# Heads of self and cross turned by DMA transposes as f16 halves, two query biases moved to ScalarE, all orders rewritten

## The chip, the cores and the metric

The kernel runs on one core of one Trainium2 chip. The metric is the device time of one execution in microseconds. TensorE (PE) multiplies, VectorE (DVE) and GpSimd (POOL) do elementwise work, ScalarE (ACT) evaluates functions, and SyncE (SP) issues the DMAs.

## The reference

Two attention blocks in a row over 64 sequences of 64 rows, width 256, 16 heads of 16. Cut to its core:

```python
# block L0: x, encoder_states = ctx
ln = layernorm(x); q, k, v = split(ln @ w_qkv + b_qkv)
x = x + merge(softmax(mask(q k / 4)) v) @ w_ao + b_ao            # "self"
q = layernorm(x) @ w_q + b_q; k, v = split(ctx @ w_kv + b_kv)
x = x + merge(softmax(mask(q k / 4)) v) @ w_co + b_co            # "cross"
x = x + gelu(layernorm(x) @ w1 + b1) @ w2 + b2                   # "mlp0"
# block L1: latents = x; keys of ctx ("ctx") and of the latents ("lat") share one softmax
h = concat([ctx, x]); q = x @ q_w + q_b; k, v = (h @ kv_w + kv_b)
y = softmax(mask(q k / 16)) v @ out_w + out_b + x                # "lat"
out = gelu(rmsnorm(y) @ mlp_w1 + mlp_b1) @ mlp_w2 + mlp_b2 + x   # "mlp1"
```

## The kernel before

The 4096 rows are cut into 32 units of 128 rows, two sequences each. Every unit goes through the same stages: self, cross, mlp0, ctx and lat, mlp1. Most large products are made of three f16 products: a matrix is kept as a high f16 half and a low f16 half (value minus high half). The weights are scaled and halved once, in the first part of the program.

Each engine has its own program, and each program is a list of stage calls written out by hand: a start (all engines fill up), a loop `for t in range(FILL, SLOTS)` and an end. One pass of the loop does each stage once, but for different units: `mix(t - 2, "self")` stands beside `hidden(t - 6, "mlp1", ...)`. The engines run these lists strictly in order and meet only at semaphores, so an instruction that waits holds up all that stands behind it on its engine. FILL is 6 before, so the loop has 26 passes.

The stages around the change, for t = self or cross, unit u:

- `mix` (PE, L609): probabilities times values into a PSUM bank. `denominators` and `divided` (DVE, L1249 and L1256) divide and write `heads_t` to SBUF as f32, 128 rows by 256 features.
- `heads_turn` (PE, L455): two f32 128x128 transposes of `heads_t` into PSUM. `heads_out` (ACT, L1823) casts the result to the high half, `heads_low` (DVE, L1156) subtracts it from PSUM and writes the low half. For lat, `heads_out` copies f32 and there are no halves.
- `project` (PE, L482; for lat L624): the turned heads times the output weight. `add_residual` (DVE, L1270, lat L1267) follows.
- `q_bias_self`, `q_bias_cross`, `q_bias_lat` (DVE, through `descaled`, L1149): query from PSUM, scale and bias, one instruction of 128x256 each. `score` (PE, L576) reads it.
- `gelu` (ACT, L1867), `hidden_hi` (ACT, L1876) and `hidden_lo` (DVE, L1276) make the halves of the hidden layer. `exponential` (ACT, L1853) makes the probabilities. Gelu and exponential use different function tables; the compiler puts an ACT_TABLE_LOAD where the program goes from one to the other.
- `across` (SP, L2498): a DMA transpose that turns a pair of f16 halves of normalized rows, `pair_t`, into `turned_t`. Before, five of them are issued for every unit (self, cross, mlp0, lat, mlp1); `load_x`, `load_rest` (four DMAs) and `store` are issued by SP too.

## Time and profile before

| | before |
|---|---|
| median of 3 runs | 1120.4 us (1119.05 to 1125.32) |
| profiled execution, device time | 1117.1 us |
| its span | 1115.1 us |
| granted TensorE clock, mean of the span | 0.991 |
| PE busy / DVE busy / ACT busy / POOL busy | 1037.7 / 982.0 / 785.7 / 633.9 us |

The span is the time from the first to the last instruction; the device time is 2.0 us more. The busy time of an engine is the union of its instructions. Ends of matmuls are modelled, so a short wait on PE can hide in busy time. In a list of waits the left side waited for the right side. In the chain that ended last, each piece is what held up the piece after it.

### The profile page before, as it was taken

How to read it: one execution, taken by the hardware profiler on the slowest of the kernel's cores; microseconds unless marked ns; L12 is line 12 of the kernel's file. 1: busy time of each engine (PE TensorE's matmuls, PEld its weight loads, DVE VectorE, ACT ScalarE, POOL GpSimd, SP SyncE). 2: the span in 40 equal slices, each digit the busy share in tenths (PEclk: the TensorE clock that was granted, in tenths of full speed). 3: DMA queues.
4: the chain of work that ended last, by engine and by line, in shares of the span. 5: the costliest groups of instructions: out<-in, count | busy, mean ns of one | idle time of the engine just before them, and what ended most of it. 6: DMA issues, size and time to landing. Idle time of an engine off the chain costs nothing.

```text
span 1115.1 us, 46381 instructions
## 1 busy us (share of the span) xinstructions
PE 1037.7 (93%) x19304; PEld 908.9 (82%) x19304; DVE 982.0 (88%) x2360; ACT 785.7 (70%) x1773; POOL 633.9 (57%) x903
## 2 busy tenths in 40 slices
PE   6677899999999999999999999999999999999997
PEld 5666678888888888888888888888888888878786
DVE  3888979989989999899999989999999999889774
ACT  2446677877667777777677777766777777666786
POOL 3866666555556565655565656555665566464421
PEclk9898999999999999999999999999999999999999
DMA  9541111122111121221111111111111122110111
GB/s 316 175 146 47 46 28 29 33 43 43 38 34 35 39 37 34 43 43 36 33 38 37 39 34 43 43 33 31 43 33 34 43 43 43 32 28 17 26 30 31
DMA packets 117473, 55.09 MB, mean 49 GB/s; under 512 B 98960, under 2 KB 115088, under 8 KB 116240
## 3 DMA queue, kind: packets, MB, share of 16 engines
q1 hardware_dynamic: 117264, 52.13, 19.4%
q8 instruction: 153, 2.51, 0.9%
q14 instruction: 56, 0.46, 0.1%
HBM read 26.93 MB, written 4.19 MB: 28 GB/s over the span
## 4 chain that ended last, share of the span: by engine, by line
PE 45%; DVE 23%; DMA 12%; ACT 10%; issue 6%; POOL 2%; SPq 1%; ACTq 0%; POOLq 0%; DVEq 0%
PE psum L469 11%; PE psum L649 10%; PE psum L609 7%; PE psum L482 6%; DMA turned_lat<-pair_lat 5%; PE psum L595 5%; DMA turned_cross<-pair_cross 4%; PE psum L576 4%; ACT staging L1867 2%; ACT hid_mlp L1867 2%; DVE prob_self L1214 2%; DVE prob_cross L1243 2%; PE psum L455 2%; DVE mx_ctx L1224 2%; DVE prob_cross L1214 1%
## 5 line engine op out<-in xcount | busy, mean ns | idle before, releaser
L2270 POOL TENSOR_TENSOR prob_self<-prob_self,add_self 128x512 f32<-128x512 f32 x64 | 90.9, 1437 | 87.8 <-DVE prob_self L1214 87.7
L2270 POOL TENSOR_TENSOR prob_cross<-prob_cross,add_cross 128x512 f32<-128x512 f32 x64 | 81.1, 1288 | 59.9 <-DVE prob_cross L1214 59.9
L2219 POOL TENSOR_TENSOR rstd_mlp<-var_mlp,minus_half 128x1 f32<-128x1 f32 x64 | 36.3, 567 | 123.1 <-DVE var_mlp L1137 89.8
L1867 ACT ACTIVATE hid_mlp<-psum,folded,undo_in 128x128 f32<-128x128 f32 x256 | 95.8, 464 | 7.2 <-PE psum L469 7.2
L1867 ACT ACTIVATE staging<-psum,cols,undo_in 128x128 f32<-128x128 f32 x256 | 96.2, 457 | 4.9 <-PE psum L469 3.9
L649 PE MATMUL psum<-hi_n,staging 128*128 128x256 f16 x512 | 94.3, 273 | 1.2 <-DVE staging L1276 1.2
L469 PE MATMUL psum<-turned_mlp,hi_m 128*128 128x128 f16 x1024 | 92.7, 219 | 2.4 <-DMA turned_mlp<-pair_mlp 2.1
L469 PE MATMUL psum<-turned_mlp,hi_n 128*128 128x128 f16 x1024 | 92.5, 219 | 0.3 <-DMA turned_mlp<-pair_mlp 0.3
L649 PE MATMUL psum<-hi_m,parts_mlp 128*128 128x256 f16 x512 | 90.1, 273 | 1.1 <-DVE parts_mlp L1276 1.1
L469 PE MATMUL psum<-turned_mlp,lo_n 128*128 128x128 f16 x512 | 88.9, 219 | 0.0
L469 PE MATMUL psum<-turned_mlp,lo_m 128*128 128x128 f16 x512 | 88.9, 219 | 0.0
L1853 ACT ACTIVATE probT_cross<-psum 128x512 f32<-128x512 f32 x64 | 35.1, 595 | 73.4 <-PE psum L595 73.3
L1853 ACT ACTIVATE late<-psum 128x512 f32<-128x512 f32 x128 | 69.7, 596 | 22.0 <-PE psum L595 21.5
L2247 POOL TENSOR_TENSOR xb<-x,rows 128x256 f32<-128x256 f32 x96 | 84.5, 881 | 0.2
L469 PEld LDWEIGHTS psum<-turned_mlp,hi_m 128*128 128x128 f16 x1024 | 76.8, 98 | 8.2 <-issue 6.6
L469 PEld LDWEIGHTS psum<-turned_mlp,hi_n 128*128 128x128 f16 x1024 | 79.6, 98 | 1.8 <-DMA turned_mlp<-pair_mlp 0.6
L2276 POOL TENSOR_TENSOR late<-late,mx_ctx 128x512 f32<-128x512 f32 x64 | 70.4, 1101 | 17.7 <-DVE mx_ctx L1230 14.8
L649 PE MATMUL psum<-lo_n,staging 128*128 128x256 f16 x256 | 69.8, 273 | 0.0
L649 PE MATMUL psum<-lo_m,parts_mlp 128*128 128x256 f16 x256 | 69.8, 273 | 0.0
L1853 ACT ACTIVATE probT_self<-psum 128x512 f32<-128x512 f32 x64 | 35.0, 595 | 44.3 <-PE psum L595 44.3
L469 PE MATMUL psum<-turned_lat,hi_side 128*128 128x128 f16 x512 | 49.6, 219 | 16.9 <-DMA turned_lat<-pair_lat 16.9
L609 PE MATMUL psum<-val_ctx,late 128*64 128x34 f32 x1024 | 62.2, 225 | 0.3 <-issue 0.3
(267 smaller groups left out, 3801.5 us busy)
## 6 DMA issues: line engine op xcount, KB each, us to landing
xin<-in_x SPq DMA_DIRECT2D x32, 128.0 KB, 2.3
late<-in_ctxT SPq DMA_DIRECT2D x4, 1024.0 KB, 7.6
ctxT<-in_ctxT SPq DMA_DIRECT2D x32, 128.0 KB, 2.1
late<-in_x SPq DMA_DIRECT2D x4, 1024.0 KB, 6.2
out<-xb SPq DMA_DIRECT2D x32, 128.0 KB, 1.9
staging<-in_w_m SPq DMA_DIRECT2D x2, 1024.0 KB, 7.2
staging<-in_w_n SPq DMA_DIRECT2D x2, 1024.0 KB, 5.2
mask<-in_mask_cross SPq DMA_DIRECT2D x32, 32.0 KB, 1.9
```

Source lines behind the costliest of these rows:

```text
L469: last = e.matmul(out_ap, wt[name][:, k, c:c + P], xs[:, k, :], start=(n == 0), stop=(n == 3 * KH - 1))
L482: last = e.matmul(ps[:, 0:H], xs[:, k, :], wt[name][:, k, c:c + H], start=(n == 0), stop=(n == 3 * KH - 1))
L576: last = e.matmul(ps[here, h * HC * S:(h + 1) * HC * S], qT["lat" if t == "ctx" else t][rows_of, h, here], spread[t][rows_of, h, :, here], ...
L595: last = e.transpose(bank[in_bank["prob_turn", t, a, u]][:, n * S:(n + 1) * S], prob[t][h][here, j * P:(j + 1) * P], ident[here, here])
L609: last = e.matmul(ps[S * a:S * a + S, p * VW:(p + 1) * VW], probT[s][a][:, j, :], val[s][:, a, p, :], start=(n == 0), stop=(n == len(sets) ...
L649: last = e.matmul(ps[:, 0:H], a, wt, start=(g == 0 and n == 0), stop=(g == 1 and n == 11))
L1853: e.activation(probT[t][a][:, :, :], src, ACT.Exp).then_inc(sem["probT_" + t], 1)
L1867: last = e.activation(hid[t][g][:, j * P:(j + 1) * P], ps[:, j * P:(j + 1) * P], ACT.Gelu_apprx_tanh, bias=b1[:, 4 * g + j:4 * g + j + 1], ...
L2219: e.tensor_tensor(rstd[t][:, :], var[t][:, :], minus_half[:, :], ALU.pow).then_inc(sem["rstd_" + t], 1)
L2247: e.tensor_tensor(o[:, :], a[:, :], row, ALU.add).then_inc(sem["plus_bias_" + t], 1)
L2270: e.tensor_tensor(ch, ch, over_heads(a[:, :]), ALU.add).then_inc(sem["added_" + t], 1)
L2276: e.tensor_tensor(ch, ch, over_keys(max_of("ctx", h)), ALU.subtract).then_inc(sem["shifted_ctx"], 1)
```

## The change

For self and cross, the heads are halved before they are turned. ACT casts `heads_t` to f16 (`heads_high`), DVE subtracts that from `heads_t` in SBUF (`heads_low`), and SP turns both halves with one DMA transpose (`heads_across`); `project` waits for that DMA. `heads_turn` and `heads_out` stay for lat alone. `q_bias_cross` and `q_bias_lat` move to ACT as two instructions each. FILL becomes 7, and every list, of start, loop and end, is written in a new order. The core of the diff, without the lists:

```diff
-FILL, SLOTS = 6, UNITS
+FILL, SLOTS = 7, UNITS
...
+        heads_pair = {t: sb("heads_pair_" + t, [P, 2, H], F16) for t in ("self", "cross")}
+        heads_turned = {t: sb("heads_turned_" + t, [P, 2, KH, P], F16) for t in ("self", "cross")}
...
                     q.wait_ge("lo_side", 1)
-                    q.wait_ge("heads_lo_" + t, u + 1)
+                    q.wait_ge("heads_across_" + t, 16 * (u + 1))
...
             def heads_low(u, t):
-                ps = bank[in_bank["heads_turn", t, u]][:, 0:KH * P].rearrange("p (k t) -> p k t", k=KH)
-                q.wait_ge("headsT_" + t, u + 1)
-                e.tensor_tensor(h_lo[t], ps, h_hi[t], ALU.subtract).then_inc(sem["heads_lo_" + t], 1)
+                q.wait_ge("heads_hi_" + t, u + 1)
+                e.tensor_tensor(heads_pair[t][:, 1, :], heads[t][:, :], heads_pair[t][:, 0, :], ALU.subtract).then_inc(sem["heads_lo_" + t], 1)
...
+            def heads_high(u, t):
+                q.wait_ge("heads_" + t, 2 * u + 2)
+                q.wait_ge("heads_across_" + t, 16 * u)
+                e.copy(heads_pair[t][:, 0, :], heads[t][:, :]).then_inc(sem["heads_hi_" + t], 1)
...
+            def q_bias_cross(u):
+                q.wait_ge("q_mm_cross", u + 1)
+                q.wait_ge("score_cross", u)
+                q.wait_ge("undone", UNDONE["out"])
+                ps = bank[in_bank["q", "cross", u]]
+                for k in range(KH):
+                    last = e.activation(qT["cross"][:, k, :], ps[:, k * P:(k + 1) * P], ACT.Identity, bias=folded[:, 6 + k:7 + k], scale=down_q[:, 1:2])
+                last.then_inc(sem["q_cross"], 1)
...
+            def heads_across(u, t):
+
+                q.wait_ge("heads_lo_" + t, u + 1)
+                q.wait_ge("proj_mm_" + t, u)
+                q.wait_ge("heads_across_" + t, 16 * u)
+                e.dma_start_transpose(heads_turned[t][:, :, :, :].rearrange("p i k t -> p (i k) t"),
+                                      heads_pair[t][:, :, :].rearrange("p i h -> p (i h)")).then_inc(sem["heads_across_" + t], 16)
```

On TensorE, in a pass in the middle of the loop, the transposes of the lat's and self's heads stood right behind the mix of self and ahead of other work. Before:

```order
L609 MATMUL psum<-val_self,probT_self 64x34 x16
L576 MATMUL psum<-spread_ctx,q_lat 64x128 x16
L455 MATMUL psum<-ident,heads_lat 128x128 x2
L455 MATMUL psum<-ident,heads_self 128x128 x2
L482 MATMUL psum<-hi_side,turned_lat 128x256 x4
L482 MATMUL psum<-lo_side,turned_lat 128x256 x2
```

After, the projection of cross comes behind `qk_self`, `v_self` (the first two rows) and two turns of probabilities; the mixes of cross and self stand some 34 rows further up:

```order
L482 MATMUL psum<-hi_qkv,turned_self 128x256 x4
L482 MATMUL psum<-lo_qkv,turned_self 128x256 x2
L596 MATMUL psum<-ident,late 128x64 x32
L482 MATMUL psum<-hi_out,heads_turned_cross 128x256 x4
L482 MATMUL psum<-lo_out,heads_turned_cross 128x256 x2
```

So the two transposes of self's heads are gone, and between the mixes and the projections stands the lat's projection, one half of `hidden`, `qk_self`, `v_self` and two `prob_turn`.

On ScalarE, one stretch of a loop pass with all gelus and the loads of function tables. Before (`staging` is the hidden layer of mlp1, `late` the scores of ctx and lat):

```order
L1867 ACT_TABLE_LOAD
L1867 ACTIVATE staging<-psum,cols,undo_in 128x128 x4
L1845 ACTIVATE val_lat<-psum,undo 64x8x16 x4
L1808 ACTIVATE xn_cross<-x,shift_cross,rstd_cross 128x256
L1876 ACTIVATE staging<-staging,hidden_up 128x512
L1867 ACTIVATE staging<-psum,cols,undo_in 128x128 x4
L1867 ACTIVATE hid_mlp<-psum,folded,undo_in 128x128 x4
L1876 ACTIVATE parts_mlp<-hid_mlp,hidden_up 128x512
L1867 ACTIVATE hid_mlp<-psum,folded,undo_in 128x128 x4
L1816 ACTIVATE pair_mlp<-xb,rstd_mlp 128x256
L1876 ACTIVATE parts_mlp<-hid_mlp,hidden_up 128x512
L1853 ACT_TABLE_LOAD
```

After, behind three gelus of the same pass:

```order
L1938 ACT_TABLE_LOAD
L1938 ACTIVATE probT_self<-psum 128x512
L1930 ACTIVATE val_lat<-psum,undo 64x8x16 x4
L1938 ACTIVATE probT_self<-psum 128x512
L1938 ACTIVATE probT_cross<-psum 128x512 x2
L1915 ACTIVATE pair_lat<-x,power 128x256
L1961 ACTIVATE staging<-staging,hidden_up 128x512
L1887 CAST heads_pair_cross<-heads_cross 128x256
L1930 ACTIVATE val_cross<-psum 64x8x16 x4
L1887 CAST heads_pair_self<-heads_self 128x256
L1952 ACT_TABLE_LOAD
L1952 ACTIVATE staging<-psum,cols,undo_in 128x128 x4
```

The exponentials of self and cross now lie between the third and the fourth gelu, so a pass has four table loads instead of two; the program has 120 instead of 68.

On SyncE, one pass of its queue. Before:

```order
L2498 DMA_TRANSPOSE turned_cross<-pair_cross 128x4x128
L2506 DMA out<-xb 128x256
L2498 DMA_TRANSPOSE turned_lat<-pair_lat 128x4x128
L2498 DMA_TRANSPOSE turned_mlp<-pair_mlp 128x4x128
L2498 DMA_TRANSPOSE turned_self<-pair_self 128x4x128
L2465 DMA xin<-in_x 128x256
L2498 DMA_TRANSPOSE turned_mlp<-pair_mlp 128x4x128
```

After:

```order
L2616 DMA xin<-in_x 128x256
L2666 DMA out<-xb 128x256
L2649 DMA_TRANSPOSE turned_self<-pair_self 128x4x128
L2649 DMA_TRANSPOSE turned_lat<-pair_lat 128x4x128
L2658 DMA_TRANSPOSE heads_turned_cross<-heads_pair_cross 128x4x128
L2658 DMA_TRANSPOSE heads_turned_self<-heads_pair_self 128x4x128
L2628 DMA ctxT<-in_ctxT 128x256
L2629 DMA mask<-in_mask_cross 128x64
L2631 DMA keys_i<-in_mask_keys 64x64 x2
L2649 DMA_TRANSPOSE turned_mlp<-pair_mlp 128x4x128 x2
L2649 DMA_TRANSPOSE turned_cross<-pair_cross 128x4x128
```

A pass has seven transposes instead of five. The loads of ctx and masks now stand behind the two turns of heads.

## Rows read from the trace of the kernel before

**Rows 1.** The page, part 1: busy time, share, instructions of each engine.

```profile
PE 1037.7 (93%) x19304; PEld 908.9 (82%) x19304; DVE 982.0 (88%) x2360; ACT 785.7 (70%) x1773; POOL 633.9 (57%) x903
```

**Rows 2.** Busy time by stretch: length, busy us (instructions) by engine, PEclk, DMA, GB/s.

```profile
200.00:1000.00 800.00, 775.15 (x14818) 682.21 (x14802) 739.39 (x1771) 587.39 (x1349) 468.43 (x649) 1.00 0.18 38
```

**Rows 3.** heads_self on VectorE, asked at 190:215 and at 1000:1035.

```profile
L1256 DVE TENSOR_TENSOR heads_self<-psum,over_self x1: 424/424/424, 199.9 to 199.9; 128x256 f32<-128x256 f32 x1
...
L1256 DVE TENSOR_TENSOR heads_self<-psum,over_self x2: 424/424/425, 1001.0 to 1028.5; 128x256 f32<-128x256 f32 x2
```

**Rows 4.** Waits of TensorE's weight load, 200:1000: us, times, longest.

```profile
PEld psum L469 <- DMA turned_lat<-pair_lat: 18.2, 12, 1.8
...
PEld psum L469 <- DMA turned_cross<-pair_cross: 10.7, 12, 1.8
...
PEld psum L455 <- DVE heads_self L1256: 0.4, 2, 0.2
```

**Rows 5.** Waits of VectorE, 200:1000.

```profile
DVE headsT_cross L1156 <- ACT headsT_cross L1823: 18.5, 12, 1.8
...
DVE headsT_self L1156 <- ACT headsT_self L1823: 7.2, 25, 0.3
...
DVE mx_lat L1224 <- PE psum L576: 0.5, 1, 0.5
```

**Rows 6.** Waits of ScalarE, 200:1000.

```profile
ACT probT_cross L1853 <- PE psum L595: 63.9, 25, 2.6
...
ACT late L1853 <- PE psum L595: 19.7, 26, 1.9
```

**Rows 7.** Chain that ended last, 560:660: start, us, what.

```profile
560.55 2.98 DMA turned_cross<-pair_cross
...
564.43 0.66 PE psum L482 x6
565.08 0.65 PE psum L595 x16
...
581.25 0.67 PE psum L469 x12
...
636.83 4.31 DMA turned_lat<-pair_lat
```

**Rows 8.** Timeline of TensorE, around 615: start, duration, instruction.

```profile
615.05 0.43 PE L455 MATMUL psum<-ident,heads_self 128*128 128x128 f32 x2
615.32 0.60 PE L482 MATMUL psum<-hi_side,turned_lat 128*128 128x256 f16 x4
```

**Rows 9.** Timeline of ScalarE, 616 to 620.

```profile
616.52 1.28 ACT L1867 ACT_TABLE_LOAD   x1
617.82 1.50 ACT L1867 ACTIVATE staging<-psum,cols,undo_in 128x128 f32<-128x128 f32 x4
619.20 1.51 ACT L1845 ACTIVATE val_lat<-psum,undo 64x128 f32<-64x128 f32 x4
```

**Rows 10.** Groups by line and shape: busy us, mean ns | idle before, releaser.

```profile
L1149 DVE SCALAR_TENSOR_TENSOR q_cross<-psum,down_q,folded 128x256 f32<-128x256 f32 x32 | 15.3, 478 | 10.9 <-PE psum L469 10.5
...
L1156 DVE TENSOR_TENSOR headsT_cross<-psum,headsT_cross 128x256 f16<-128x256 f32 x32 | 13.6, 424 | 23.4 <-ACT headsT_cross L1823 21.8
...
L1146 DVE TENSOR_TENSOR pair_mlp<-xn_mlp,pair_mlp 128x256 f16<-128x256 f32 x32 | 24.2, 757 | 1.3 <-POOL pair_mlp L2228 1.3
...
L1830 ACT ACTIVATE pair_lat<-x,power 128x256 f16<-128x256 f32 x32 | 16.3, 510 | 1.8 <-DVE x L1286 1.8
...
L1823 ACT CAST headsT_cross<-psum 128x256 f16<-128x256 f32 x32 | 11.9, 372 | 50.7 <-PE psum L455 50.6
...
L1867 ACT ACT_TABLE_LOAD x34 | 43.6, 1283 | 0.6
```

**Rows 11.** Timeline of SyncE's queue: start, time of the issue.

```profile
638.12 2.39 SPq L2498 DMA_TRANSPOSE turned_mlp<-pair_mlp  x1
```

**Rows 12.** Tile turned_lat: time to landing over 32 transposes.

```profile
DMA to landing us min/median/max: 2.4/2.5/4.6
```

More of the change, by code:

```diff
@@ new lines, in _ @@
+            total(0, "n2", 5)
+            q_cross(2, 3)
+            project(1, "cross", 1)
+            score(2, "cross", 2)
+            hidden(0, "mlp0", 1, 4)
+            outward(0, "mlp0", 0, 7)
+            qk_self(5, 2)
+            k_cross(3, 5)
+            outward(0, "mlp0", 1, 7)
+            prob_turn_bank(2, "cross", 1)
+            mix(4, "self", 6)
+            prob_turn(2, "cross", 7)
+            project(3, "self", 4)
+            score_bank(5, "self", 2)
+            score(5, "self", 0)
@@ L762, in _ @@
+            mix(2, "cross", 4)
+            hidden(1, "mlp0", 0, 2)
+            hidden(1, "mlp0", 1, 7)
+            q_lat(0, 4)
+            score_bank(0, "ctx", 2)
+            k_lat(0, 6)
+            score(0, "ctx", 4)
+            v_self(5, 0)
+            v_cross(3, 1)
             score_bank(0, "lat", 4)
             score(0, "lat", 2)
-            total(0, "n2", 1)
-            q_cross(3, 6)
-            project(2, "cross", 0)
-            outward(1, "mlp0", 0, 1)
+            k_ctx(1, 6)
@@ new lines, in _ @@
+            v_self(UNITS - 1, 0)
+            q_cross(UNITS - 2, 2)
+            score_bank(UNITS - 1, "self", 4)
+            score(UNITS - 1, "self", 6)
+            heads_turn(UNITS - 5, "lat", 1)
+            score_bank(UNITS - 2, "cross", 2)
+            score(UNITS - 2, "cross", 4)
+            hidden(UNITS - 6, "mlp1", 0, 1)
+            k_lat(UNITS - 4, 6)
+            v_ctx(UNITS - 4, 3)
+            hidden(UNITS - 3, "mlp0", 0, 0)
+            project(UNITS - 5, "lat", 2)
+            hidden(UNITS - 3, "mlp0", 1, 7)
@@ L1952, in _ @@
             exponential(0, "lat", 1)
-            exponential(4, "self", 1)
+            normalize(2, "mlp0")
+            exponential(3, "cross", 0)
+            heads_out(0, "lat")
+            exponential(3, "cross", 1)
+            q_bias_lat(1)
+            values(1, "ctx")
             gelu(2, "mlp0", 0)
+            heads_high(3, "cross")
+            hidden_hi(2, "mlp0", 0)
+            gelu(2, "mlp0", 1)
+            hidden_hi(2, "mlp0", 1)
             values(1, "lat")
-            heads_out(0, "lat")
@@ L2006, in _ @@
-            heads_out(UNITS - 5, "lat")
-            gelu(UNITS - 6, "mlp1", 1)
+            values(UNITS - 4, "ctx")
+            gelu(UNITS - 3, "mlp0", 0)
+            gelu(UNITS - 3, "mlp0", 1)
+            exponential(UNITS - 1, "self", 0)
+            exponential(UNITS - 1, "self", 1)
+            hidden_hi(UNITS - 3, "mlp0", 0)
+            hidden_hi(UNITS - 3, "mlp0", 1)
+            exponential(UNITS - 2, "cross", 0)
+            heads_high(UNITS - 1, "self")
+            exponential(UNITS - 2, "cross", 1)
@@ L2016, in _ @@
[L2016 to L2023 removed]
+            normalize(UNITS - 1, "cross")
+            q_bias_lat(UNITS - 3)
+            gelu(UNITS - 6, "mlp1", 1)
+            normalize(UNITS - 2, "mlp0")
```

1865 lines of the change are left out of this document (988 added, 877 removed).

## The prediction

> **What bounds the kernel now.** I read the shares first: PE 93%, DVE 88%, ACT 70%, POOL 57% [rows 1]. Shares mix the start, where weights are loaded and halved, with the loop, so next came the stretch 200 to 1000, which is nothing but the loop, at full granted clock (1.00, the 2.4 GHz level): PE busy 775.2 of 800 us, DVE 739.4, ACT 587.4 [rows 2]. The reader should see that two engines are nearly full and a third is not.
>
> The length of a pass is read from one instruction that occurs once in it. heads_self starts at 199.9 for one unit and at 1001.0 for the unit 25 passes on [rows 3]: 801.1 / 25 = 32.04 us a pass. The other 314 us of the span are start and end.
>
> What would a pass be without waits? The waits by engine answer that. TensorE's weight load waited for others in six groups, from 18.2 to 0.4 us and 39.4 in all, 1.58 a pass; the two largest, together 28.9, are for the DMA transposes of the lat's and of cross's rows [rows 4]. That leaves 32.04 - 1.58 = 30.46 us of PE. DVE waited 43.3 us in five groups, 18.5 to 0.5, so 1.73 a pass; its own work is 30.31. Most of that waiting is heads_low for ACT, 18.5 and 7.2 [rows 5]. ACT waited 205 us in six groups from 63.9 to 19.7 and a last one of 0.2, so 8.2 a pass, and holds 23.84 us of work [rows 6]. So a pass of 32.04 is a PE of 30.5 and a DVE of 30.3, both in written order, plus about 1.6 us that PE loses, mostly to landings. The chain shows what such a landing is: 2.98 us from the end of DVE's low half for cross at 560.55, but 4.31 for the lat's at 636.83 [rows 7], where the next transpose stands right behind and its issue took 2.39 us [rows 11]. Over all 32, the lat's landed in 2.4 to 4.6 us, median 2.5 [rows 12]. That median counts from the issue's end, the chain's pieces from its start.
>
> **The change part by part, per pass.**
>
> TensorE. Two pairs of f32 transposes go. One pair occupies from 615.05 to 615.32, where the next matmul starts [rows 8]: 0.27 us, not the 0.43 shown, since matmuls overlap. Two pairs are 0.54, and PE's own work falls from 30.46 to 29.92. No other product changes.
>
> VectorE. Two query biases of 478 ns go [rows 10]: -0.96, less a little because neighbours overlap, which I leave out. heads_low now has two SBUF inputs in place of one in PSUM. Its old form took 424 ns; the nearest rows of the new form are the low halves of normalized rows, of which mlp0's take 757 ns [rows 10]. So it costs between nothing and 2 x 0.33 = 0.67; I take 0.35, as POOL is busy little over half the time. DVE's work is then 30.31 - 0.96 + 0.35 = 29.7 (29.35 to 30.0). The 757 ns row stands at a place where POOL adds rows at the same time. The Trainium skill, SBUF — State Buffer, section Who interferes with whom, says that a DVE instruction with two SBUF inputs contends with a GpSimd instruction that reads SBUF; by it alone either bound could come out, depending on what POOL does then, so the sum goes by the rows.
>
> ScalarE. Two more table loads: the load at 616.52 is followed by the gelu at 617.82, so 1.30 each, 2.60 in all [rows 9]. Four bias instructions of 128x128 from PSUM, with scale and bias from SBUF: a gelu of the same shape and operands goes four in 1.38 us (617.82 to 619.20) [rows 9]; I take 1.38, and 2.04 as the upper bound at the 510 ns of pair_lat, which has more columns. Below 1.38 I see no reason. Two heads_high at 510 replace two casts of 372: +0.28 [rows 10]. Sum 23.84 + 2.60 + 1.38 + 0.28 = 28.1, at most 28.8. That is hidden under PE's 29.9 if ACT waits for no more than 1.8 us a pass, where it now waits 8.2. So this cover is thin: three engines of 29.9, 29.7 and 28.1 have to mesh.
>
> The table loads are the place where a rule speaks against the change. The Trainium skill, ScalarE: Activation LUTs, section What ACT_TABLE_LOAD costs, has 1283 ns for the load and about 1380 for a drain, 2.66 for each switch. The trace has the 1283 [rows 10] and, from load to next gelu, 1.30 with no further gap. By the page's figure two more switches would be an estimated 5.3 us and ACT the bound at 30.9 before any wait; by the row they are 2.6.
>
> The new wait. project now waits for a DMA. Behind it on PE stand q_lat and all else; so what matters is the work between mix and project. For self it is, by the order, the lat's projection, 24 matmuls of hidden, 24 of qk_self, v_self, two turns of probabilities, cross's projection and q_lat. 12 such matmuls take 0.67, six of 256 columns 0.66, a turn of probabilities 0.65 [rows 7]: 4 x 0.67 + 2 x 0.66 + 2 x 0.65 + 0.67 = 6.0, without the lat's projection. The chain to be hidden is reciprocal and divide (about 0.7, an estimate from the 424 ns form and a small one before it), heads_high 0.51, heads_low 0.42 to 0.76, and the landing at 2.98 to 4.31: 4.6 to 6.3. Usual landings are hidden; a slow one just about. The two heads' transposes lie back to back in SP's list, the pattern that gave 4.31. Cross is first there and has the same distance.
>
> Old landings. The DMAs that PE waited for get room. lat_low stands in DVE's new list ahead of the division of cross's heads, so it is done when the mix of cross is; q_lat comes on PE only behind the lat's projection, 48 matmuls of hidden and qk_self, v_self, two turns and cross's projection: over 5.3 us by the same rows. Cross's rows are turned at the end of DVE's pass and q_cross stands behind 48 hidden matmuls of the next, 2.7 us. load_rest's four DMAs now stand behind the heads' and not in front of lat's and cross's. So of the 28.9 us / 25 = 1.16 a pass I expect 1.0 to go and 0.15 to stay. The other 0.42 (10.5 us / 25) are waits for ACT and DVE; I let them stay, as those two engines get fuller relative to PE.
>
> Pass after: 29.92 + 0.15 + 0.42 = 30.5. If DVE takes its upper bound 30.0, this still holds.
>
> SP. Seven transposes at no more than the 2.39 us of a blocked one [rows 11] are under 17 us of issue in a pass of 30: no bound, but each waits in line.
>
> Start and end. Seven units' share of transposes lies there: 7 x 0.54 = -3.8. At the end nothing covers the landings of the last self and cross heads: each replaces 0.27 + 0.37 by 2.98 and more, about +2.5, so +5. FILL 7 moves one pass from the loop into the written-out start; it is one pass of the same work. I cost the new order of the first loads at nothing, with 10 us either way as its bound.
>
> **Sum.** 25 x (30.5 - 32.04) = -38.5; -3.8 + 5 = +1.2. Span 1115.1 - 37.3 = 1077.8; the device time is 2.0 more, 1079.8. The profiled execution was 3.3 below the median of the runs, whose three values spread over 6 us; I stay with **1080**.
>
> **The rivals.**
>
> 1. Half a gain (chance 0.22). In-order engines at 29.9, 29.7 and 28.1 don't mesh: a late exponential or a late q_bias holds up PE, or slow landings of the seven transposes go on. For it: ACT's 1.8 us of room, the 4.31. Against: DVE's waits for headsT, 25.7 us of its 43.3, are gone. With a pass of 31.2: 25 x 0.84 = 21; 1117.1 - 21 + 1 = 1097.
> 2. All waits go (0.07). Pass 29.9: 25 x 2.14 = 53.5; 1117.1 - 53.5 + 1 = 1065.
> 3. The gain doesn't arrive (0.06). New waits eat all that old ones gave back, pass 32.0: 1117 to 1122. This would be the change that doesn't do what it says: landings late as before, only of heads in place of lat's.
> 4. Slower (0.07). ACT becomes the bound, by the split of gelus and exponentials. If ACT has its upper 28.8 and keeps half of its present 8.2 us of waits, since it must wait in order for PE's turns of probabilities, a pass is 32.9 and the time 1117.1 + 25 x 0.86 + 1 = 1139. It decides from 32.04 - 28.1 = 3.9 us of ACT waiting a pass on. Against it: in the new order exponentials stand behind several pieces of ACT work that can be done meanwhile. The skill's 2.66 per switch (same page as above) would push the same way, to an estimated pass of 32 to 33; the trace has no such drain at either kind of switch.
>
> The forecast itself, 1066 to 1094, has 0.58.
>
> **How the numbers follow.** A measurement of this kernel can tell about 0.5% (5.6 us) from no change. Forecast, rival 1 and rival 2 are faster: 0.87. Rival 3 is the same: 0.06. Rival 4 is slower: 0.07. The range 1062 to 1106 leaves out rivals 3 and 4 (0.13), the upper part of rival 1 and little below; it holds the start's 10 us either way around 1080 and the pass between 29.9 and 31.5.
>
> **What the profile after would show.** Right: L455 with lat alone, 64 instead of 192 transposes; a pass of 30.2 to 30.8 us by the same instruction's starts; PE's waits for turned_lat and turned_cross under 5 us each in the loop; ACT busy near 910 (785.7 + 67 + 44 + 9) with 120 table loads of 1.28; DVE busy near 960; heads_low between 0.42 and 0.76. Wrong in part: project (L482) waiting for heads_turned by more than 10 us in the loop, which says slow landings; PE waiting for probT or late (L1938) by more than 25, which is rival 1 or 4 by ACT. Wrong altogether: a gap of over 1 us behind each table load, or a start longer by over 10 us than 200 us less one pass's gain, which the loop could not make good.

## The result, and the profile after

| | before | after |
|---|---|---|
| median | 1120.28 us (1119.05 to 1125.32, 4 runs) | 1105.09 us (1103.1 to 1106.9, 4 runs) |
| profiled execution, span | 1115.1 us | 1104.4 us |

The ratio is 0.9856, 95% interval 0.9819 to 0.9892: faster by 15 us, where 40 were forecast. The time lies in the range, 1 us from its slow end, and 8 us behind rival 1 (half a gain, 1097), whose pass of 31.2 us it has.

The page, part 1, and the share of each engine in the chain that ended last:

```profile
PE 1025.0 (93%) x19176; PEld 900.7 (82%) x19176; DVE 977.4 (88%) x2296; ACT 909.0 (82%) x1953; POOL 633.4 (57%) x903
...
DVE 37%; PE 24%; ACT 22%; issue 12%; POOL 3%; DMA 2%; SPq 0%; DVEq 0%; ACTq 0%; POOLq 0%
```

The loop's busy time by stretch (length, busy us and instructions by engine, granted clock, DMA share, GB/s):

```profile
200.00:1000.00 800.00, 781.65 (x15127) 689.22 (x15124) 758.80 (x1761) 710.72 (x1535) 479.12 (x662) 1.00 0.23 46
```

The same instruction as in [rows 3], asked at 190:950:

```profile
L1269 DVE TENSOR_TENSOR heads_self<-psum,over_self x25: 410/411/411, 196.4 to 946.5; 128x256 f32<-128x256 f32 x25
```

25 starts are 24 passes: 750.1 / 24 = 31.25 us, against 32.04 [rows 3]. TensorE's busy time went from 31.04 to 30.53 us a pass (775.15 / 800 x 32.04 and 781.65 / 800 x 31.25): the transposes are gone as priced. A pass of 30.5 was forecast, and 0.79 us of the 1.54 came.

Where is the rest? Waits of TensorE, its weight load (PEld) and VectorE, 200:1000 (us in all, times, longest), which answer to [rows 4, 5]:

```profile
PE psum L576 <- ACT q_lat L1897: 15.8, 25, 0.8
```
```profile
PEld psum L596 <- DVE prob_cross L1256: 6.3, 25, 0.3
...
PEld psum L482 <- DMA heads_turned_cross<-heads_pair_cross: 0.8, 3, 0.3
```
```profile
DVE spread_lat L1202 <- PE psum L469: 9.9, 25, 0.6
DVE late L1220 <- PE psum L576: 9.5, 26, 0.6
```

The weight load's waits for landings, 28.9 us before, are 0.8 us in all. In their place TensorE waits for ScalarE, 15.8 us at one instruction, in each pass. VectorE has 22.5 us of waits for others left in six groups, 0.88 a pass (800 / 31.25 = 25.6 passes), so its own work is 31.25 - 0.88 = 30.4 us: as much as TensorE's, and 0.7 more than forecast.

The chain that ended last shows how a pass goes round (start, us, what):

```profile
602.64 0.42 DVE heads_self L1269
...
603.51 1.28 ACT L1952
...
604.81 1.50 ACT staging L1952 x4
...
606.33 1.26 ACT L1938
...
608.61 0.97 ACT late L1938 x2
609.59 0.71 ACT q_lat L1897 x2
...
610.50 0.70 PE psum L576 x32
611.19 1.99 PE psum L610 x64
...
616.20 0.68 PE psum L469 x12
...
616.91 0.48 DVE spread_lat L1202
617.39 1.25 DVE staging L1289
```

From 617.39 all is VectorE, with short pieces that the profile puts under "issue", up to the next heads_self at 633.88. So a pass is one cycle of 31.2 us: some 17 on VectorE, 7 on ScalarE (603.07 to 610.29) and 6.5 on TensorE. Of ScalarE's seven, 4.1 are a table load, a gelu and a table load. No engine is full by itself.

On VectorE two instructions of this cycle had become dear: of the latents' two low halves of the hidden layer (L1289, `staging`) one, at 617.31, takes 1336 ns and the other still 742, and the low half of cross's heads takes 960. Groups by line and shape, 200:1000 (busy us, mean ns):

```profile
L1289 DVE SCALAR_TENSOR_TENSOR staging<-staging,hidden_up 128x512 f16<-128x512 f32 x52 | 53.0, 1020 | 0.0
...
L1184 DVE TENSOR_TENSOR heads_pair_cross<-heads_cross,heads_pair_cross 128x256 f16<-128x256 f32 x25 | 24.0, 960 | 0.0
...
L1184 DVE TENSOR_TENSOR heads_pair_self<-heads_self,heads_pair_self 128x256 f16<-128x256 f32 x25 | 10.6, 425 | 3.4
```

And before, the first of them:

```profile
L1276 DVE SCALAR_TENSOR_TENSOR staging<-staging,hidden_up 128x512 f16<-128x512 f32 x50 | 37.0, 739 | 0.0
```

The low half of cross takes 960 ns in the mean (987 in the median) and that of self, the same form, 425. The timelines of VectorE and of GpSimd show what runs beside it:

```profile
601.73 0.99 DVE L1184 TENSOR_TENSOR heads_pair_cross<-heads_cross,heads_pair_cross 128x256 f16<-128x256 f32 x1
```
```profile
601.71 0.73 POOL L2376 TENSOR_TENSOR xb<-x,rows 128x256 f32<-128x256 f32 x1
602.40 0.91 POOL L2376 TENSOR_TENSOR x<-x,rows 128x256 f32<-128x256 f32 x1
```

### The profile page after: what moved, and what is told of

It reads as the page before. It is cut to its first block, busy times and chain, and to the rows that moved or that the text cites. A ratio compares the mean times of both kernels' runs of the same rounds, so it can differ in the third digit from the quotient of the medians.

```text
span 1104.4 us, 46419 instructions
## 1 busy us (share of the span) xinstructions
PE 1025.0 (93%) x19176; PEld 900.7 (82%) x19176; DVE 977.4 (88%) x2296; ACT 909.0 (82%) x1953; POOL 633.4 (57%) x903
## 4 chain that ended last, share of the span: by engine, by line
DVE 37%; PE 24%; ACT 22%; issue 12%; POOL 3%; DMA 2%; SPq 0%; DVEq 0%; ACTq 0%; POOLq 0%
PE psum L610 6%; PE psum L650 5%; ACT staging L1952 4%; PE psum L469 4%; ACT L1952 4%; PE psum L576 4%; ACT L1938 3%; DVE prob_self L1256 3%; DVE mx_lat L1237 3%; DVE mx_cross L1237 3%; DVE staging L1289 3%; ACT late L1938 3%; PE psum L482 3%; DVE mx_self L1237 3%; DVE prob_cross L1227 3%
## 5 line engine op out<-in xcount | busy, mean ns | idle before, releaser
L2399 POOL TENSOR_TENSOR prob_cross<-prob_cross,add_cross 128x512 f32<-128x512 f32 x64 | 91.4, 1447 | 78.4 <-DVE prob_cross L1227 78.2
L2405 POOL TENSOR_TENSOR late<-late,mx_ctx 128x512 f32<-128x512 f32 x64 | 67.3, 1051 | 117.2 <-DVE mx_ctx L1243 117.0
L2399 POOL TENSOR_TENSOR prob_self<-prob_self,add_self 128x512 f32<-128x512 f32 x64 | 80.4, 1273 | 56.1 <-DVE prob_self L1227 55.8
L650 PE MATMUL psum<-hi_m,parts_mlp 128*128 128x256 f16 x512 | 93.7, 272 | 1.4 <-DVE prob_cross L1227 0.9
L469 PE MATMUL psum<-turned_mlp,hi_m 128*128 128x128 f16 x1024 | 90.1, 219 | 0.0
L1938 ACT ACTIVATE late<-psum 128x512 f32<-128x512 f32 x128 | 72.2, 599 | 2.8 <-PE psum L596 2.5
L2376 POOL TENSOR_TENSOR xb<-x,rows 128x256 f32<-128x256 f32 x96 | 71.0, 742 | 4.9 <-DVE x L1283 4.2
L1289 DVE SCALAR_TENSOR_TENSOR staging<-staging,hidden_up 128x512 f16<-128x512 f32 x64 | 62.0, 969 | 5.5 <-ACT staging L1961 5.3
L650 PEld LDWEIGHTS psum<-hi_n,staging 128*128 128x128 f16 x512 | 50.0, 98 | 18.6 <-issue 9.5
```

Source lines behind the costliest of these rows:

```text
L469: last = e.matmul(out_ap, wt[name][:, k, c:c + P], xs[:, k, :], start=(n == 0), stop=(n == 3 * KH - 1))
L650: last = e.matmul(ps[:, 0:H], a, wt, start=(g == 0 and n == 0), stop=(g == 1 and n == 11))
L1289: e.scalar_tensor_tensor(part[t][g][:, 512:1024], hid[t][g][:, :], hidden_up[t], part[t][g][:, 0:512], ALU.mult, ALU.subtract).then_inc(se ...
L1938: e.activation(probT[t][a][:, :, :], src, ACT.Exp).then_inc(sem["probT_" + t], 1)
L2376: e.tensor_tensor(o[:, :], a[:, :], row, ALU.add).then_inc(sem["plus_bias_" + t], 1)
L2399: e.tensor_tensor(ch, ch, over_heads(a[:, :]), ALU.add).then_inc(sem["added_" + t], 1)
```

## The experiments

The theory was: the loop is now set by this cycle, through (a) the two extra table loads on ScalarE and (b) VectorE's instructions with two SBUF inputs that GpSimd stretches. The rivals: the landings, TensorE's own work, or one engine alone. A second question came with the results: what each part of the change is worth. "Pass" is the mean distance of two heads_self starts in 190:950, from the profile of each run. Each ratio is to the kernel before as timed with that run (medians 1118.3 to 1118.9 us; 1120.3 for the change).

| run | median us | ratio to before, 95% interval | pass us |
|---|---|---|---|
| the change | 1105.09 | 0.9856 (0.9819 to 0.9892) | 31.25 |
| e1_one_switch | 1097.66 | 0.9806 (0.9780 to 0.9833) | 30.82 |
| e2_pool_order | 1124.29 | 1.0051 (1.0031 to 1.0070) | 32.10 |
| e7_pool_gap | 1099.08 | 0.9835 (0.9795 to 0.9876) | 30.92 |
| e8_and_hidden_lo | 1096.93 | 0.9824 (0.9783 to 0.9866) | 30.89 |
| e9_and_one_switch | 1092.22 | 0.9775 (0.9741 to 0.9808) | 30.59 |
| e12_act_order | 1112.60 | 0.9942 (0.9923 to 0.9961) | 31.45 |
| e13_start_order | 1108.18 | 0.9908 (0.9882 to 0.9935) | 31.45 |
| e15_low_and_start | 1094.01 | 0.9784 (0.9764 to 0.9804) | 30.87 |
| e17_values_first | 1086.75 | 0.9720 (0.9699 to 0.9741) | 30.60 |
| e3_q_bias_before | 1136.77 | 1.0156 (1.0131 to 1.0181) | 32.60 |
| e6_q_bias_back | 1145.79 | 1.0242 (1.0219 to 1.0265) | 32.80 |
| e16_q_bias_back_late | 1129.06 | 1.0095 (1.0069 to 1.0121) | 32.12 |
| e14_dma_in_old_order | 1215.11 | 1.0844 (1.0799 to 1.0889) | 35.32 |
| e10_heads_on_pe | 1140.35 | 1.0199 (1.0164 to 1.0233) | 32.63 |
| e11_heads_on_pe_bank2 | 1103.44 | 0.9868 (0.9839 to 0.9897) | 31.16 |
| e18_pe_low_and_start | 1100.90 | 0.9849 (0.9827 to 0.9871) | 31.16 |

### The cycle: table loads and GpSimd

**e1.** In the changed kernel (this leaves the gelu out for half of the latents' hidden layer, so its outputs are not the reference's; the same holds for e9):

```diff
-ps[:, j * P:(j + 1) * P], ACT.Gelu_apprx_tanh,
+ps[:, j * P:(j + 1) * P], ACT.Identity if (t, g) == ("mlp1", 1) else ACT.Gelu_apprx_tanh,
```

> The changed kernel, with Identity in place of gelu for the second half of the latents' MLP (so the outputs aren't the reference's): it needs no gelu table there, and the two extra table loads of a pass (2.57 us of ScalarE) go; everything else stays. Theory (those two loads lie on the cycle VectorE, ScalarE, TensorE, VectorE that sets the pass of 31.25 us): the pass falls by 2.57 us or to the next bound, which is VectorE's own work, 30.4 us: pass 30.4 to 30.6, time 1083 to 1090. Rival (the loads are hidden, as the prediction assumed, and VectorE or the landings set the pass): pass 31.2, time 1102 to 1107.

Measured: pass 30.82, 0.43 us less, 7 us in all. The loads are on the cycle, but only 0.43 of their 2.57 us came back. The chain says what stood right behind them:

```profile
600.34 0.56 POOL rstd_mlp L2348
...
600.98 0.12 ACT pair_mlp L1874
...
601.40 1.06 ACT late L1938 x2
```

ScalarE's pair_mlp stands among the exponentials and waits for GpSimd's root (10.5 us in 300:900, 19 times). Removing a piece of a cycle shows the next one, here 0.43 us below.

**e2.** On GpSimd, the two additions that ran beside the low half of cross go behind the bias of self:

```diff
-                plus_bias(t - 4, "lat")
-                plus_bias(t - 5, "mlp1")
                 root(t, "self")
                 plus_bias(t - 1, "self")
+                plus_bias(t - 4, "lat")
+                plus_bias(t - 5, "mlp1")
```

> The changed kernel with two GpSimd additions of a pass (the bias rows onto the latents' and the MLP's x) issued behind the bias of self instead of ahead of the root of self, so that they don't run while VectorE writes the low half of the cross heads. Theory (that subtraction takes 960 ns instead of the 424 ns of its twin of self because GpSimd works beside it, and it lies on the cycle): it falls to 450 to 550 ns and the pass by 0.4 to 0.5 us, time 1092 to 1096. Rival (the 960 ns are the shape's own price): still 960 ns, pass 31.2. Rival (VectorE isn't on the cycle): it falls, and the pass doesn't.

The group by shape in 200:1000, and the wait that came, in 300:900:

```profile
L1184 DVE TENSOR_TENSOR heads_pair_cross<-heads_cross,heads_pair_cross 128x256 f16<-128x256 f32 x24 | 10.2, 423 | 0.0
```
```profile
DVE x L1283 <- POOL xb L2376: 14.1, 18, 0.8
```

The half fell from 960 to 423 ns, so GpSimd's work beside it was the cause and not its shape (e7, which moves the same two additions elsewhere, has 423 ns too). But the time rose by 19 us against the change: the two additions now stood ahead of the residual that VectorE needs and of the root, and VectorE waited 0.78 us a time for it. The size of the stretch was right, the expected time wrong.

**e7.** The same two additions in GpSimd's idle gap instead:

```diff
                 mask_add(t - 1)
+                plus_bias(t - 4, "lat")
+                plus_bias(t - 5, "mlp1")
                 root(t - 3, "mlp0")
```

> The changed kernel with the two GpSimd additions for the latents and their MLP moved to where GpSimd is idle for 1.5 us anyway, behind the mask of the next pass, ahead of the root of the MLP. The run with them behind the bias of self had the low half of the cross heads at 424 ns instead of 987, but made GpSimd late for a residual and for a root. Theory (VectorE's stretched instruction lies on the cycle): 424 ns again, no new wait for GpSimd, pass 30.6 to 30.8, time 1088 to 1094. Rival (the cycle runs past it through ScalarE and its table loads): pass 31.1 to 31.25, time 1100 to 1106.

423 ns and no wait for GpSimd. Pass 30.92: 0.33 of the 0.54 us came, and 1099.08 us lies between the time expected and the rival's. The chain shows why: the cycle now leaves VectorE at the heads of cross and goes past its low half, through ScalarE's cross values (597.68 0.27 ACT val_cross L1930).

**e8.** On top of e7, on VectorE: `hidden_lo(t - 8, "mlp1", 1)` from the head of the loop to behind `hidden_lo(t - 7, "mlp1", 0)`, for unit t - 7.

> As the run before (label e7_pool_gap), and the low half of the latents' second hidden group moved on VectorE from 617.3 us, where GpSimd works beside it and it takes 1336 ns, to behind the low half of the first group at 613.5, where GpSimd is idle. Theory: it falls to about 745 ns, VectorE's wait of 0.4 us for TensorE ahead of the latents' keys is filled too, pass 30.1 to 30.5, time 1075 to 1087. Rival (what is pushed back by it, the next unit's masked scores and the additions on GpSimd behind them, is late for VectorE): pass as in e7 or longer.

```profile
L1289 DVE SCALAR_TENSOR_TENSOR parts_mlp<-hid_mlp,hidden_up,parts_mlp 128x512 f16<-128x512 f32 x52 | 49.9, 960 | 0.0
L1289 DVE SCALAR_TENSOR_TENSOR staging<-staging,hidden_up 128x512 f16<-128x512 f32 x52 | 36.6, 742 | 0.0
```

The instruction moved fell to its old 742 ns, but its twin of mlp0 rose from 766 to 960. One of mlp0's two now lies beside GpSimd's low half of ctx:

```profile
614.22 1.15 DVE L1289 SCALAR_TENSOR_TENSOR parts_mlp<-hid_mlp,hidden_up,parts_mlp 128x512 f16<-128x512 f32 x1
```
```profile
613.84 0.99 POOL L2340 TENSOR_TENSOR ctx_lo<-ctxT,ctx_hi 128x256 f16<-128x256 f32 x1
```

The stretch was moved, not removed, and the pass stayed (30.89). That is a miss of the expectation, and the rival (what it pushes back) was nearer.

**e9.** e8 with the edit of e1.

> As e8_and_hidden_lo, and Identity in place of gelu for the second half of the latents' MLP (so the outputs aren't the reference's), which takes away two of the four table loads of a pass. Theory (VectorE's cover is gone, so ScalarE's table loads matter more than in the first such run, where they were worth 0.43 us a pass): 0.3 to 0.5 us a pass below e8_and_hidden_lo, down to TensorE's own 29.9 at the least, time 1067 to 1080. Rival (hidden now): as e8_and_hidden_lo.

0.30 us a pass and 5 us less than e8, at the lower end of the step expected (1092.22 us is outside the time expected, since e8 itself came out higher): the two loads are still on the cycle, and again only a part of their 2.57 us comes back.

**e12.** On ScalarE, on top of e8:

```diff
+                values(t - 2, "cross")
                 heads_high(t - 3, "cross")
-                values(t - 2, "cross")
...
-                scaled_high(t - 6)
...
                 exponential(t - 5, "lat", 1)
+                scaled_high(t - 6)
```

and `low_pair(t - 6, "mlp1")` behind `low_pair(t - 3, "mlp0")` on VectorE.

> As e8_and_hidden_lo (pass 30.89 us), with ScalarE's order changed at two places: the values of cross ahead of the high half of the cross heads (where ScalarE stood 1.0 us for those heads), and the high half of the latents' MLP input behind the four exponentials, with its low half on VectorE two places later. Theory (the cycle runs now from the cross heads through ScalarE, with val_cross 1.13 us, one table load, gelu, one table load and the exponentials, to the queries of the latents): it gets shorter by 0.5 to 1.0 us on ScalarE, pass 30.2 to 30.5 (TensorE's own work is 30.0), time 1081 to 1088. Rival (VectorE or TensorE binds by itself at 30.9): 1094 to 1099.

Slower than e8 by 16 us, outside both expectations. The chain:

```profile
616.83 0.64 ACT xn_mlp L1865
...
617.53 0.41 POOL pair_mlp L2356
...
617.96 0.43 DVE pair_mlp L1175
...
618.78 0.30 DVE late L1220
```

The high half, moved back, made ScalarE's normalized rows of mlp0 late, those GpSimd's cast, and that VectorE's low half, with the masks of ctx behind it.

**e17.** So the good half of it alone, on e15 (below), and VectorE's order to match:

```diff
-                heads_high(t - 3, "cross")
                 values(t - 2, "cross")
+                heads_high(t - 3, "cross")
...
-                heads_low(t - 3, "cross")
                 divided(t - 2, "self")
+                heads_low(t - 3, "cross")
```

> As e15_low_and_start, with ScalarE's values of cross ahead of the high half of the cross heads (where ScalarE stands 1.0 us), and VectorE's self heads ahead of the low half of the cross heads; the MLP input's high half stays among the exponentials, where e12_act_order had moved it and made VectorE late. Theory (the cycle runs through ScalarE's val_cross, 1.13 us, ahead of the table load): the loads start 0.4 to 0.6 us earlier, pass 30.4 to 30.6, time 1081 to 1086. Rival (the landing of the cross heads, whose low half is now 0.4 us later, becomes a wait of TensorE): pass 30.9 or more, 1092 to 1097.

1086.75 us, the fastest of all: ratio 0.9720 to before, 18 us below the change and 7 below e15. Pass 30.60, at the upper bound of what was expected, and the time 1 us above it. Its largest wait of VectorE in 300:900 and its chain (TensorE's waits for ScalarE are 0.2 us in all there):

```profile
DVE x L1283 <- PE psum L482: 13.1, 19, 0.7
```
```profile
603.56 5.53 PE psum L469 x96
...
609.72 2.73 PE psum L650 x24
...
619.91 1.06 PE psum L625 x4
620.97 2.68 PE psum L469 x48
```

From 603.56 to 628.32, and on to 656.83, the chain is nothing but TensorE; ahead of it VectorE stands for the 8 us from 595.70. The engine that the prediction had as the bound is nearly the bound again, at a pass 0.1 us above the 30.5 forecast, once the other two are out of its way. ScalarE is not in this chain, although its four table loads are still there.

### What each part of the change is worth

**e3.** The biases alone, in the kernel before's loop: on ScalarE `q_bias_cross(t - 2)` behind `gelu(t - 3, "mlp0", 1)` and `q_bias_lat(t - 3)` behind self's normalized rows, and off VectorE.

> The kernel before, with the biases of q_cross and q_lat in the loop on ScalarE instead of VectorE, and nothing else of the change. The prediction's account (VectorE's work is hidden before, TensorE and the landings set the pass of 32.04 us): pass 31.7 to 32.2, time 1115 to 1122. Rival (VectorE's 0.95 us count in full): pass 31.1, time 1097. Rival (ScalarE is late with q and TensorE waits for it): pass 32.3 to 33, time 1127 to 1144.

18 us slower, pass 32.60: in the range of the third expectation, but by another wait than it named. In 300:900:

```profile
DVE parts_mlp L1276 <- ACT parts_mlp L1895: 24.7, 19, 2.3
DVE headsT_cross L1156 <- ACT headsT_cross L1821: 14.5, 9, 1.8
```

Not TensorE waits for q, but VectorE for ScalarE, for what now stands behind the biases in ScalarE's list (TensorE's wait for q_cross is 0.3 us). So this run doesn't tell what the biases are worth in the old order, only that they don't go in without a new one.

**e6 and e16.** The changed kernel with both biases back on VectorE: cross's behind `shifted(t - 2, "self", 1)`, the latents' ahead of `add_residual(t - 3, "cross")` in e6 and behind `add_residual(t - 2, "self")` in e16.

> The changed kernel, with the biases of q_cross and q_lat in the loop back on VectorE, the other parts of the change kept. VectorE gets 0.95 us more work in a pass, ScalarE 1.38 us less. Theory (VectorE's own work of 30.4 us is just below the pass of 31.25 us; the cycle runs through both engines, and takes 0.48 more on VectorE and 0.65 less behind ScalarE): VectorE then becomes the bound alone with 31.35, pass 31.3 to 31.6, time 1106 to 1114. Rival (only VectorE's work counts): pass 32.2, time 1128. Rival (ScalarE alone is the bound): pass 30 to 30.6, time 1075 to 1090.

> As e6_q_bias_back, where VectorE stood 0.85 us a pass for the latents' query product, because I had put its bias too early; here it stands two residuals later, when that product is done. So this run tells what the two biases are worth by themselves in the new order. Theory (VectorE's own work sets the pass: 30.4 + 0.95 = 31.35 us, and a little for its other waits): pass 31.4 to 31.8, time 1108 to 1120. Rival (most of the loss of that run came from the biases themselves): pass 32.3 or more, 1130 or more.

e6 had a wait of my own making (0.88 us a time, 200:1000):

```profile
DVE q_lat L1178 <- PE psum L469: 21.9, 25, 1.7
```

Without it (e16) the pass is 32.12, 0.87 above the change and 24 us in all, and 0.3 above what I expected. VectorE's own work is 31.5 there (15.4 us of waits in 25 passes, 0.62). But its chain is nearly all TensorE, and TensorE stands twice in every pass: for the latents' query from VectorE (12.0 us in 200:1000), and 1.24 us ahead of the scores of cross (30.0 us, 24 times). The profile puts the second under "issue"; it ends 0.1 us behind the end of VectorE's q_cross:

```profile
634.34 0.47 DVE L1178 SCALAR_TENSOR_TENSOR q_cross<-psum,down_q,folded 128x256 f32<-128x256 f32 x1
```
```profile
634.92 0.70 PE L576 MATMUL psum<-spread_cross,q_cross 32*64 32x128 f32 x32 [1.24 <-issue]
```

So in both runs cross's bias, too, stood too late in VectorE's list (e6 has the same 1.24 us, 29.4 in all). They show that the biases can't simply go back into the new lists; what the 0.95 us of VectorE's work costs by itself they don't show.

**e14.** The DMA transposes alone, in the kernel before's order:

```diff
-                heads_turn(t - 2, "self", 4)
-                heads_turn(t - 2, "cross", 7)
...
                 load_x(t)
+                heads_across(t - 2, "self")
...
                 across(t - 5, "mlp1")
+                heads_across(t - 2, "cross")
```

> The kernel before, with the heads of self and cross turned by DMAs in the loop (units 4 to 29) and everything else as it was: its orders, the biases on VectorE. The projections follow the heads too closely for it: between the mix of self and its projection TensorE has 2.1 us of other work, between the mix of cross and its projection 4.5 us, and a landing took 2.4 to 4.6 us, with about 1.3 us on VectorE and ScalarE ahead of it. Theory: TensorE waits 2 to 4 us more for self and 0 to 2 us more for cross in each pass, less the 0.54 us: pass 34 to 37, time 1165 to 1250. Rival (the landings are hidden in any order): pass 31.5, time 1107.

96 us slower, pass 35.3. TensorE's waits, 200:1000:

```profile
PE psum L492 <- DMA headsT_self<-heads_pair_self: 51.7, 23, 2.9
PE psum L492 <- DMA headsT_cross<-heads_pair_cross: 23.3, 18, 3.2
```

In the old lists the DMAs cost 96 us: the new ones are what makes them possible.

**e10 and e11.** The reverse: the changed kernel, its order and biases, with the heads turned by TensorE in the loop, `heads_turn(t - 3, "cross", 3)` behind the latents' projection and `heads_turn(t - 2, "self", ...)` behind the second half of `hidden`, into bank 6 in e10 and bank 2 in e11; ScalarE's and VectorE's halves are moved to where the turned heads are ready, and with them ScalarE's values of cross go ahead of cross's high half (one of the two moves of e17), its gelu ahead of self's high half, and VectorE's self heads ahead of cross's low half (the other move of e17).

> The changed kernel with the heads of self and cross turned by TensorE again in the loop (units 5 to 29 and 4 to 28; the start and the end keep the DMAs), ScalarE copying the high half and VectorE taking the low half out of PSUM, as before the change; the new orders and the two biases on ScalarE stay. TensorE gets 0.54 us more work in a pass, VectorE's low halves fall from 960 and 425 ns to 424 each. Theory (TensorE is not the bound, VectorE is): pass 30.8 to 31.3, time 1093 to 1106, no slower than with the DMAs. Rival (the prediction's: TensorE's work and its waits are what counts): pass 31.8 to 32.3, time 1120 to 1130.

> As e10_heads_on_pe, where TensorE had turned the self heads into bank 6, which the next unit's values need right after, and stood 1.4 us a pass for VectorE to empty it. Here they go to bank 2, which is free until the latents' queries 4 us later. So this run has the new orders and the two biases on ScalarE, and TensorE's turning in the loop. Theory (VectorE sets the pass, and the DMAs' own part of the change gives nothing, since it takes 0.54 us from TensorE and puts 0.56 us on VectorE): pass 30.9 to 31.4, time 1095 to 1109, as the changed kernel. Rival (TensorE's work counts): pass 31.8 or more, time 1120 or more.

e10 is a miss of mine: the next values needed bank 6 (24.8 us of waiting for heads_turned_self in 300:900). e11's time is that of the change, 1103.44 against 1105.09, intervals overlapping. Its stretch in the loop, and its chain:

```profile
200.00:1000.00 800.00, 790.71 (x15264) 700.25 (x15258) 751.85 (x1765) 713.01 (x1538) 476.68 (x664) 1.00 0.18 38
```

```profile
600.03 1.05 issue
601.08 0.04 ACT heads_turned_cross L1912
...
601.47 1.28 ACT L1981
...
614.42 5.41 PE psum L482 x96
```

TensorE is busy 30.80 us of 31.16 a pass, VectorE's halves cost 424 ns each out of PSUM. The time is as expected, but not by the theory: VectorE isn't in this chain at all. The cycle goes round ScalarE (599.46 to 608.52) and TensorE, and ScalarE stands 1.05 us in each pass for the turned heads of cross, which TensorE takes up only behind the latents' projection. So equal times don't say that the DMAs are worth nothing: e11 has e17's two moves, which gave 7 us where the DMAs do the turning, and pays for a wait that the DMAs don't have.

**e18 against e15.** The two kernels once more, with hidden_lo moved (e8) and the start's loads (e13) in both; e15 has e7's move on GpSimd too; the half that it relieves comes out of PSUM in e18.

> e8_and_hidden_lo (pass 30.89 us, 1096.9) with the start's loads as in e13_start_order, which was 4.4 us shorter than its twin by them. Theory (start and loop add up): loop as in e8, time 1090 to 1094. Rival (the start's gain is lost again ahead of the loop): 1096 to 1098.

> e11_heads_on_pe_bank2 (heads of self and cross turned by TensorE in the loop, pass 31.17 us) with the two moves of e15_low_and_start that apply to it: hidden_lo where GpSimd is idle, and the start's loads. TensorE's own work is 31.0 us a pass here, 30.5 with the DMAs. Theory (with VectorE's stretch gone the DMAs are worth something at last): the pass stays at 31.0 to 31.2, and the time 3 to 7 us above e15_low_and_start, 1095 to 1100. Rival (DMAs worth nothing here either): the same time as e15_low_and_start.

e18 stays at 31.16 and 1100.90; e15 is at 30.87 and 1094.01, 7 us less, and their intervals are apart. e18 also has e17's two moves, which e15 lacks, so e17 is the nearer twin: 30.60 and 1086.75, 0.56 us a pass and 14 us below e18. That is the 0.54 forecast for the transposes, but it isn't shown to be theirs alone: e18's chain goes through ScalarE as e11's does, with the same wait for the turned heads of cross (19.8 us in 300:900), and e18 lacks e7's move on GpSimd. So with the DMAs the loop can be 7 to 14 us shorter than with TensorE's turns as they were placed here; how much of that is the DMAs' own stays open.

### The start

**e13.** On e12, the loads:

```diff
-            load_tile(0, "out")
             load_x(0)
             load_weight(0, "qkv")
             load_columns(0)
+            load_tile(0, "out")
```

and on TensorE `squared_tile(0, "out", 5)` behind `fold_rest(0, "qkv", 1)`.

> As e12_act_order, with the start's order of loads partly undone: the output projections' weights behind the columns instead of first of all, and their sums on TensorE behind those of the first weight. Theory (TensorE stood 9.1 us at the start for the columns, 6.0 in the kernel before): it stands 6 us, and the start becomes 1 to 3 us shorter. Rival (something else of the start is late by as much): nothing gained. The loop is that of e12_act_order.

TensorE's wait in 0:196, in e12 and in e13:

```profile
PE psum L371 <- DMA cols<-in_cols: 9.2, 1, 9.2
```
```profile
PE psum L371 <- DMA cols<-in_cols: 6.1, 1, 6.1
```

4.4 us less in the medians, and e15 is 2.9 below e8 by the same edit: the first thing that TensorE needs was loaded behind half a megabyte (two weights of 256 KB) that it needs later.

## Why the prediction was too fast

The direction and the range held, and so did the mechanism in part: the old landings went and the transposes came off TensorE. The size didn't hold, since TensorE wasn't what set the pass. By its own steps, per pass:

| step | forecast | measured |
|---|---|---|
| TensorE, two pairs of transposes | -0.54 | -0.51 busy |
| TensorE's own work, pass less its waits for others | 29.92 | 30.27 |
| landings that stay | 0.15 | 0.03 (0.8 us in 25.6 passes) |
| ScalarE's work | 28.1 | 28.2 (31.25 less 78.5 / 25.6 of waits) |
| table load to gelu | 1.30 | 1.30 (603.51 to 604.81) |
| VectorE's work | 29.7, at most 30.0 | 30.4 |
| TensorE's other waits | 0.42 | 0.62 for q_lat, 0.25 for prob_cross, and 0.08 in small groups |
| pass | 30.5 | 31.25 |
| start and end, us in all | +1.2, 10 either way | +9 (span -10.7, loop 25 x -0.79) |

**The step that failed** is "Pass after: 29.92 + 0.15 + 0.42 = 30.5. If DVE takes its upper bound 30.0, this still holds." It took the pass as TensorE's own work plus old waits, and let the waits for ACT and DVE stay because they were small before. The runs put in its place: with the landings gone, the loop is a cycle through three engines, and TensorE waits for whichever is late on it. The waits for ACT and DVE, left at 0.42, became 0.95. Another 0.35 of the missing 0.75 shows up in no wait with a name: the weight load's gaps that the profile puts under "issue" grew from 32.4 to 59.3 us in 200:1000, in part the same wait for q_lat; the rest of them stays open. That the meshing is what was missing, e17 shows: with the same parts in a better order the pass is 30.60. Two things made it 31.25.

- VectorE's work, the mis-sized term. heads_low was priced at 0.35 for both (bound 0.67); it cost 0.54, all of it cross's, which alone went past the 0.33 that bounded one of them (960 ns against the 757 of the row), and self's nothing. The sum left out what GpSimd does to instructions that the change doesn't touch but moves: the latents' two low halves of the hidden layer rose from 739 to a mean of 1020 ns (one of them to 1336), 0.56 a pass, against 0.34 that mlp0's low half gave back (757 [rows 10] to 416). 30.31 - 0.96 + 0.54 + 0.56 - 0.34 = 30.1; the last 0.3 is mostly self's shifted scores (L1256, 659 to 750 ns, twice a pass) and a mean of squares (L1159, 220 to 421 ns). e2 and e7 show the cause for cross's half, e8 for the latents' one; for the last two it wasn't tested.
- ScalarE's cover. "Hidden under PE's 29.9 if ACT waits for no more than 1.8 us a pass" failed: ACT waited 3.07 (78.5 us in nine groups). That number alone proves little, since it is what a pass of 31.25 leaves of 28.2 us of work, whoever sets the pass; TensorE's 15.8 us for q_lat and the runs e1 and e9 say it. Its work was sized right in all (the casts of the high halves took 405 ns, not 510). The two switches were worth 0.43 and 0.30 us a pass in e1 and e9, so they are neither hidden nor a full 2.57.

TensorE's wait for q_lat was foreseen in words as rival 1, "a late q_bias holds up PE", with the weight 0.22; it was nearer the truth than the forecast. Its other half, slow landings, is out: 0.8 us. Rival 4 (ACT alone the bound) is out too, as ACT's waits stayed under the 3.9 us from which it decides. The Trainium skill, ScalarE: Activation LUTs, section What ACT_TABLE_LOAD costs, has a drain of about 1380 ns beside the load; by it two more switches would be an estimated 5.3 us. The trace disagrees: the gelu starts 0.02 us behind the end of the load, 1.30 us from its start (603.51, 604.81), and the exponential behind the next load likewise (606.33, 607.62). (The 30.9 that the prediction got by this figure is 30.8 by its own terms.) The Trainium skill, SBUF — State Buffer, section Who interferes with whom, says that VectorE's instructions with two SBUF inputs contend with GpSimd's reads; e2 agrees, with 960 ns against 423. The prediction had this rule and priced it by POOL's mean share; which POOL instruction lies beside which is in the two orders and the timelines.

**Start and end** were costed at +1.2 with 10 us either way for the start, and came out 9 us longer than the loop's gain leaves. The heads_self of the same unit comes 3.5 us earlier than before at the loop's start (196.4 against 199.9), and from the last heads_self to the end it is 13.0 us longer (1004.8 to 1104.4 against 1028.5 to 1115.1). Part of that is work moved: TensorE is busy 10.2 us less in the first stretch and 10.2 more in the last, as the new lists put more of the units' work behind this instruction. In idle time of TensorE the start lost 6.7 us and the end 2.8. Of the start's, 3 to 4 are the columns' later landing (e13, e15); the rest was not taken apart.

**What the parts are worth.** None of them stands by itself: biases alone +18 us (e3), DMAs alone +96 (e14), orders and biases without the DMAs -15 (e11, with moves of its own in the lists), orders and DMAs without the biases +11 (e16, with cross's bias late). Each of these runs carries a wait that its own placing made, so their times don't price the parts. The prediction's ledger had the transposes' 0.54 as its first term; in the changed kernel it shows in TensorE's busy time and not in the pass, where the cycle lies elsewhere.

Still open: what the biases are worth by themselves in the new lists, and how much of the new orders' own worth would show with neither biases nor DMAs, which no run had.

## What to carry to other kernels

When several in-order engines each have nearly a full pass of work (here 30.5, 30.4 and 28.2 us of 31.25), the pass can be a cycle through all of them, not the busiest one's work plus its waits: take the chain's one repeated loop, and price an edit only where it lies on that loop. When a part is taken out again to price it, look in that run's chain for a wait that the new placing made, before its time is called the part's worth. After removing the largest wait, ask which of the other waits stand within a few tenths behind it, since that is the gain's ceiling. Read in the two orders, side by side, what GpSimd does while VectorE runs each instruction with two SBUF inputs: moving two GpSimd additions (e2, e7) or one VectorE instruction (e8) changed such instructions by a factor of 1.8 to 2.3.

## What the runs showed of the hardware

- The same VectorE subtraction, 128x256 f32 from two SBUF tiles to f16, takes 423 ns alone and 985 to 993 ns beside GpSimd additions of the same size (300:900; e2 and e7 against the change). A 128x512 one takes 742 ns alone and 1336 beside GpSimd's additions and scaling (at 617.31), and one of mlp0's 1.15 us beside GpSimd's subtraction (e8). Not every overlap costs as much: in the changed kernel one of mlp0's takes 0.78 us (624.63) beside GpSimd's additions of 128x512 (623.59 to 626.54).
- From the start of an ACT_TABLE_LOAD to the start of the next ACTIVATE it is 1.29 to 1.30 us in the chain, in either direction between gelu and exponential, also four times a pass: no further gap.
- SyncE's seven transposes a pass landed 2.4 to 4.5 us behind their issue in 200:1000, with medians of 2.4 to 2.9 by tile, and the weight load waited 0.8 us in 25.6 passes for them: in this order the DMA queue wasn't the bound.
